# Cross-attention of 64 keys in parts of the matmul array: half-width scores, paired transposes, contexts in 64x64 quarters

## The chip, the cores and the metric

The kernel runs on one core of one Trainium2 chip. The metric is the device time in microseconds (us) of one execution. Engines are named as in the profile: PE is TensorE's matmul, PEld its weight load, DVE is VectorE, ACT is ScalarE, POOL is GpSimd, and SP is SyncE, which issues most DMAs.

## What is computed

The input x has 128 batches of 64 tokens with 128 features, and the context has the same shape. Each token of a batch attends to the context rows of its own batch, causally; then a mixture of experts follows (two of eight experts by a router, and one shared expert).

```
x = x + attention(layernorm(x), ctx, ctx)         # per batch: 64 queries, 64 keys, D = 128
    scores = q @ k.T * D ** -0.5;  masked above the diagonal;  softmax;  @ v
x = x + ffn(layernorm(x))
    logits = xt @ gate_w.T;  idx = top_k(logits + beta, 2);  weight = sigmoid(logits[idx])
    routed: sum over the two of weight * (silu(xt @ gate) * (xt @ up)) @ down
    shared: (silu(xt @ shared_gate) * (xt @ shared_up)) @ shared_down
```

## The kernel before

The 8192 tokens are worked in 16 groups of 512. A group is GT = 4 tiles of P = 128 tokens, so each tile holds two batches of T = 64. Each engine has its own program, a loop over iterations `it` in which it takes one step of several groups at once, and the engines meet only through semaphores. A semaphore `s_name` counts groups. In one iteration TensorE does, in this order (L1310 on): up matmul 0 of the shared expert of group it-4 (L1202), `attend(it-2)` (L1144), `transpose_xn2(it-3)` (L1154), gate matmul 0 (L1193), `transpose_probs(it-1)` (L1133), `route(it-3)` (L1163), `transpose_xn(it)` (L1113), the shared down projection of it-5 (L1214), up matmul 1 (L1202), `score(it)` (L1121, L1125), `ranks(it-3)` (L1174 to L1180) and gate matmul 1 (L1193).

Attention goes through these steps. `score` first puts a mask of 128x512 into PSUM bank A by a bf16 matmul with the identity, then adds four f32 matmuls of 128 tokens by 128 keys. Each tile of 128 tokens is so scored against both of its batches' keys, and the mask sets the other batch's half to -1e30. DVE takes the negative maximum of each row (L752), ACT the exponentials with their sums (L618). TensorE transposes the four 128x128 blocks of `probs` into bank C, ACT copies the 512 columns to `probs_T` (L626), and `attend` multiplies each by the 128 context rows of its tile into bank O. DVE's `residual` (L767) scales by the inverse sum and adds x. Router logits L and ranks R lie in bank O beside the contexts, at other times. `route` waits for the residual of the group that was attended in the same iteration (L1159), as it writes into bank O.

On DVE the residual stands behind `sum_up` and `shifts`, and ahead of the second layer norm's statistics. On ACT the exponentials stand behind the normalisation of a group two further back (L592).

SP loads a group's x, its context with features on the partitions (`c_T`, from a transposed copy in HBM) and its context rows (`c_sb`), three iterations ahead of use, in rings of 5 and 4 buffers (`load_x`, `load_c`); the contexts' buffers come free by `s_attended`. Then it stores a finished group. Routed tokens are scattered to lists by expert pair in HBM (GpSimd, L458). After the 16 groups a second stage gathers tiles of these lists and multiplies them with their experts (L1275, L1299).

A plain matmul of f32 is two instructions of each kind in the profile, so `score` has 8 besides the mask and `attend` 8. A transpose is one.

## Time and profile before

| | us |
|---|---|
| median of 3 runs | 423.53 (419.73 to 426.79) |
| the profiled execution, its own time | 422.82 |
| its span | 421.1 |
| PE busy, share of the span | 394.0, 94% |
| DVE busy | 300.8, 71% |
| ACT busy | 254.3, 60% |
| POOL busy | 267.0, 63% |

The page divides the span into 40 slices and gives each engine's busy share in tenths, and the clock that TensorE was granted, in tenths of 2.4 GHz. A timeline row merges instructions of one line; its first column is the start of the first and its second the time from there to the end of the last. As matmuls overlap, the distance from one row's start to the next row's start tells what an operation takes on the engine.

### The profile page before, as it was taken

To read this page: it belongs to the slowest core of one execution; us is meant where nothing else is said; L and a number is where in the kernel's file an instruction comes from. 1 tells how busy PE (TensorE), PEld (TensorE's weight loads), DVE (VectorE), ACT (ScalarE), POOL (GpSimd) and SP (SyncE) were. 2 spreads that over 40 slices of the span, in tenths; PEclk is the share of its full clock that TensorE was granted. 3 is DMA by queue.
4 is the path that set the end of the run, shared out by engine and by line. 5 is a ranking of instruction groups with operands and counts; after the bars stand their busy time and mean duration, and the time that the engine had idled before them with its cause. 6 is when DMAs were issued, how large, how long until landed. Compare 5 with 4: busy or idle time off the path is not lost.

```text
span 421.1 us, 10737 instructions
## 1 busy us (share of the span) xinstructions
PE 394.0 (94%) x3056; PEld 350.1 (83%) x3056; DVE 300.8 (71%) x1324; ACT 254.3 (60%) x554; POOL 267.0 (63%) x312
## 2 busy tenths in 40 slices
PE   7668999999999999989999999999999999999970
PEld 3556787778778887669999999989999999999970
DVE  3498799998999988776986666556667666666650
ACT  2568899999999994346566556553122565665520
POOL 7658788888888866617887888875200045555551
PEclk9699999999999999999999999999999999999995
DMA  8943344677444121244555666673332123432221
GB/s 241 342 126 102 102 126 127 214 239 229 126 131 156 59 60 58 73 116 98 92 82 81 91 82 91 90 111 55 50 78 55 35 26 47 53 39 26 22 25 12
DMA packets 61480, 41.76 MB, mean 99 GB/s; under 512 B 5688, under 2 KB 56384, under 8 KB 61424
## 3 DMA queue, kind: packets, MB, share of 16 engines
q1 hardware_dynamic: 49296, 30.69, 26.4%
q0 software_dynamic: 12128, 10.40, 17.4%
q8 instruction: 26, 0.43, 0.4%
q14 instruction: 30, 0.25, 0.2%
HBM read 24.17 MB, written 16.90 MB: 98 GB/s over the span
## 4 chain that ended last, share of the span: by engine, by line
PE 81%; POOL 4%; issue 4%; DVE 4%; DMA 3%; ACT 1%; SPq 1%; POOLq 0%; DVEq 0%; ACTq 0%
PE gu_pair L1275 30%; PE bank L1299 15%; PE bank L1202 7%; PE bank L1214 6%; PE bank L1193 6%; PE gu_pair L1144 3%; PE gu_pair L1125 3%; PE gu_pair L1163 3%; PE bank L1241 2%; PE gu_pair L1154 2%; DMA tile_in<-sorted_rows 1%; PE gu_pair L1113 1%; PE gu_pair L1133 1%; PE gu_pair L1180 1%; POOL rstd L417 1%
## 5 line engine op out<-in xcount | busy, mean ns | idle before, releaser
L509 POOL DMA_INDIRECT out<-t_out,tile_in x64 | 100.1, 1564 | 88.2 <-DVE t_out L1047 76.8
L1275 PE MATMUL gu_pair<-tile_T,W_slot 128*128 128x128 f32 x1024 | 124.8, 275 | 0.0
L1275 PEld LDWEIGHTS gu_pair<-tile_T,W_slot 128*128 128x128 f32 x1024 | 119.5, 192 | 0.1
L683 ACT ACTIVATE t_silu<-gu_pair 128x512 f32<-128x512 f32 (+1 forms) x78 | 46.4, 594 | 104.3 <-PE gu_pair L1275 96.2
L1007 DVE TENSOR_TENSOR t_hid<-t_silu,gu_pair 128x512 f32<-128x512 f32 (+1 forms) x78 | 53.0, 680 | 48.3 <-PE gu_pair L1275 47.9
L1299 PE MATMUL bank<-W_down,t_hid 128*128 (+1 forms) x620 | 82.7, 276 | 0.2 <-DVE t_hid L1007 0.2
L458 POOL DMA_INDIRECT sorted_rows<-rows,slot x64 | 63.6, 994 | 23.4 <-issue 16.8
L673 ACT ACTIVATE W_slot<-W 128x512 f32 x128 | 73.0, 621 | 6.1 <-issue 4.6
L1299 PEld LDWEIGHTS bank<-W_down,t_hid 128*128 128x128 f32 x620 | 75.4, 192 | 1.0 <-issue 0.8
L469 POOL DMA_INDIRECT left_in<-sorted_rows,left_index x27 | 26.5, 981 | 16.1 <-DVE left_index L926 8.2
L417 POOL TENSOR_TENSOR rstd<-var_eps,minus_half 128x4 f32<-128x4 f32 x32 | 33.0, 1032 | 5.7 <-DVE var_eps L738 5.3
L1202 PE MATMUL bank<-xn_T,shared_gu 128*128 128x512 f32 x64 | 33.2, 600 | 1.3 <-ACT silu_g L650 1.3
L592 ACT ACTIVATE rows<-x,shift,rstd 128x128 f32<-128x128 f32 x64 | 26.4, 483 | 13.0 <-DVE shift L744 13.0
L1193 PE MATMUL bank<-xn_T,shared_gu 128*128 128x512 f32 x64 | 33.2, 600 | 0.0
L1214 PE MATMUL bank<-shared_dn,hid 128*128 128x128 f32 x256 | 31.5, 276 | 0.9 <-DVE acc L845 0.9
L1214 PEld LDWEIGHTS bank<-shared_dn,hid 128*128 128x128 f32 x256 | 29.9, 192 | 1.5 <-issue 1.5
L1275 PE MATMUL gu_pair<-tile_T,W 128*128 128x128 f32 x216 | 26.4, 275 | 0.0
L424 POOL TENSOR_SCALAR xn<-x_sb,moments,rstd 128x128 f32<-128x128 f32 x32 | 25.2, 792 | 1.7
L618 ACT ACTIVATE probs<-gu_pair,neg_max 128x128 f32<-128x128 f32 x64 | 22.5, 364 | 4.9 <-DVE neg_max L752 4.8
L1275 PEld LDWEIGHTS gu_pair<-tile_T,W 128*128 128x128 f32 x216 | 25.2, 192 | 0.0
L767 DVE SCALAR_TENSOR_TENSOR x<-gu_pair,inv_sum,x_sb 128x128 f32<-128x128 f32 x64 | 18.0, 344 | 9.8 <-PE gu_pair L1144 9.8
L1241 PE MATMUL bank<-ident,tile_in 128*128 128x128 f32 x91 | 23.0, 276 | 1.7 <-DMA tile_in<-sorted_rows 1.7
(153 smaller groups left out, 637.0 us busy)
## 6 DMA issues: line engine op xcount, KB each, us to landing
tile_in<-sorted_rows SPq DMA_DIRECT2D x91, 66.5 KB, 2.0
x_sb<-x SPq DMA_DIRECT2D x16, 256.0 KB, 4.6
c_T<-ctx_cols SPq DMA_DIRECT2D x16, 256.0 KB, 2.9
c_sb<-ctx SPq DMA_DIRECT2D x16, 256.0 KB, 3.4
out<-acc SPq DMA_DIRECT2D x16, 256.0 KB, 3.4
sorted_rows<-padding SPq DMA_DIRECT2D x1, 2128.0 KB, 9.4
sorted_rows<-left_in SPq DMA_DIRECT2D x27, 66.5 KB, 2.1
sorted_rows<-rows,slot POOLq DMA_INDIRECT x64, 3.6
```

The lines of the kernel that those rows point to most:

```text
L417: e.tensor_tensor(rstd[:, n, g % 2], var_eps[:, n], minus_half[:], ALU.pow).then_inc(s_rstd[n], 1)
L458: e.indirect_dma_start(sorted_rows, bass.IndirectOffsetOnAxis(ap=slot[:, g % RR, i:i + 1], axis=0), rows[:, g % RR, i, :], None).then_inc( ...
L509: e.indirect_dma_start(out_flat, bass.IndirectOffsetOnAxis(ap=tile_in[:, tiles_of(i)[0] % NR, ID:ID + 1].bitcast(I32), axis=0), t_out[:, q ...
L673: r = e.activation(W_slot[:, q % TX, h], W[:, bass.ds(experts[q][h] * WN, WN)], ACT.Copy)
L683: e.activation(t_silu[:, 0:n * M], gate_up_pair[i % 2][0][:, 0:n * M], ACT.Silu).then_inc(s_t_silu, 1)
L1007: e.tensor_tensor(t_hid[:, i % 2, 0:n * M], t_silu[:, 0:n * M], gate_up_pair[i % 2][1][:, 0:n * M], ALU.mult).then_inc(s_t_hid, 1)
L1193: e.matmul((G0, G1)[m], shared_gu[:, 0, m * P:(m + 1) * P], xn2_T[:, g % RT], start=True, stop=True).then_inc(s_gate[m], 1)
L1202: e.matmul((U0, G0)[m], shared_gu[:, 1, m * P:(m + 1) * P], xn2_T[:, g % RT], start=True, stop=True).then_inc(s_up[m], 1)
L1214: r = e.matmul(Y[:, i * D:(i + 1) * D], hid[:, g % 2, m, i * P:(i + 1) * P], shared_dn[:, m], start=(m == 0), stop=(m == MC - 1), skip_gro ...
L1241: r = e.transpose(tile_pair[i % 2][:, h * P:(h + 1) * P], tile_in[:, n % NR, 0:D], ident[:])
L1275: r = e.matmul(bank[:, c:c + P], w, tile_T[:, i % TX, tile], start=True, stop=True, skip_group_check=True)
L1299: r = e.matmul(y, t_hid[:, i % 2, c:c + P], w, start=(m == 0), stop=(m == MC - 1), skip_group_check=True)
```

## The change

The code makes use of the batches of 64. Scores of a tile are computed for its own batch's 64 keys only: two matmuls per tile, of 64 tokens each, that write the lower and the upper 64 partitions of the same 64 columns, so that bank A holds 128x256 and the mask has 256 columns. ACT writes the exponentials so that tiles i and i+2 lie side by side in 128 columns, and one transpose turns both: two per group, into columns 0 to 255 of bank C, which ACT copies. A transposed block has the keys of tile n on partitions 0 to 63 and those of tile n+2 on 64 to 127. `attend` multiplies 64 keys by 64 tokens with 128 features, eight times: row half c of the array writes bank O (c = 0) or bank C (c = 1), and column half b the partitions of batch b. Context rows are loaded by two DMAs, each to 64 partitions. As bank C now holds contexts in the columns that the transposes write, `transpose_probs(g)` waits for the residual of group g-1.

```diff
-    ctx_rows = ctx_in.rearrange("b s d -> (b s) d").rearrange("(g t p) d -> g p t d", g=G, t=GT)
+    ctx_rows = ctx_in.rearrange("(g c m) k d -> g c k m d", g=G, c=2)
-        mask = sb("mask", [P, GT, P], BF16)
+        mask = sb("mask", [P, GT, T], BF16)
-        probs = sb("probs", [P, GT, P])
+        probs = sb("probs", [P, GT // 2, 2, T])
-        probs_T = sb("probs_T", [P, GT, P])
+        probs_T = sb("probs_T", [P, GT // 2, P])
-        L = O[:, 0:GT * E]
-        R = O[:, P:P + GT * Q]
+        scores = A[:, 0:GT * T]
+        attended = [half[:, c * 2 * D:(c + 1) * 2 * D] for c, half in enumerate((O, C))]
+        L = O[:, 2 * P:2 * P + GT * E]
+        R = O[:, 3 * P:3 * P + GT * Q]
...
-                e.dma_start(c_sb[:, g % RC], ctx_rows[g]).then_inc(s_c_in[g % RC], 16)
+                for c in range(2):
+                    e.dma_start(c_sb[c * T:(c + 1) * T, g % RC], ctx_rows[g, c]).then_inc(s_c_in[g % RC], 16)
...
-            e.affine_select(out=mask[:], in_=mask[:], compare_op=ALU.is_ge, fill=MASKED, base=0,
-                            pattern=[[0, GT], [-1, P]], channel_multiplier=1).then_inc(s_const, 1)
-            e.wait_ge(s_const, 7)
-            e.memset(mask[T:P, :, 0:T], MASKED).then_inc(s_const, 1)
+            e.affine_select(out=mask[0:T], in_=mask[0:T], compare_op=ALU.is_ge, fill=MASKED, base=0,
+                            pattern=[[0, GT], [-1, T]], channel_multiplier=1).then_inc(s_const, 1)
+            e.affine_select(out=mask[T:P], in_=mask[T:P], compare_op=ALU.is_ge, fill=MASKED, base=0,
+                            pattern=[[0, GT], [-1, T]], channel_multiplier=1).then_inc(s_const, 1)
...
-                    r = e.activation(probs[:, i], S[:, i], ACT.Exp, bias=neg_max[:, i:i + 1],
+                    r = e.activation(probs[:, i % 2, i // 2], S[:, i], ACT.Exp, bias=neg_max[:, i:i + 1],
...
-                r = e.activation(probs_T[:, :, :].rearrange("p t k -> p (t k)"), C, ACT.Copy)
+                r = e.activation(probs_T[:, :, :].rearrange("p n k -> p (n k)"), C[:, 0:GT * T], ACT.Copy)
...
-                    r = e.scalar_tensor_tensor(out=x2[:, g % RG, i], in0=O[:, i * D:(i + 1) * D],
+                    r = e.scalar_tensor_tensor(out=x2[:, g % RG, i], in0=attended[i // 2][:, i % 2 * D:(i % 2 + 1) * D],
...
-                e.matmul(A, ident_bf[:], mask[:, :, :].rearrange("p t k -> p (t k)"),
+                e.matmul(scores, ident_bf[:], mask[:, :, :].rearrange("p t k -> p (t k)"),
                          start=True, stop=False, skip_group_check=True)
                 for i in range(GT):
-                    s = slice(i * P, (i + 1) * P)
-                    r = e.matmul(A[:, s], xn_T[:, s], c_T[:, g % RC, s], start=False, stop=True, skip_group_check=True)
+                    for b in range(2):
+                        s = slice((2 * i + b) * T, (2 * i + b + 1) * T)
+                        r = e.matmul(scores[b * T:(b + 1) * T, i * T:(i + 1) * T], xn_T[:, s], c_T[:, g % RC, s],
+                                     start=False, stop=True, skip_group_check=True)
...
                 if g:
                     e.wait_ge(s_probs_T, g)
-                for i in range(GT):
-                    r = e.transpose(C[:, i * P:(i + 1) * P], probs[:, i], ident[:])
+                    e.wait_ge(s_x2, g)
+                for n in range(GT // 2):
+                    r = e.transpose(C[:, n * P:(n + 1) * P], probs[:, n].rearrange("p t k -> p (t k)"), ident[:])
...
-                e.wait_ge(s_c_in[g % RC], 16 * (g // RC + 1))
+                e.wait_ge(s_c_in[g % RC], 32 * (g // RC + 1))
...
-                for i in range(GT):
-                    r = e.matmul(O[:, i * D:(i + 1) * D], probs_T[:, i], c_sb[:, g % RC, i], start=True, stop=True)
+                for n in range(GT // 2):
+                    for b in range(2):
+                        for c in range(2):
+                            half = slice(c * T, (c + 1) * T)
+                            r = e.matmul(attended[c][b * T:(b + 1) * T, n * D:(n + 1) * D],
+                                         probs_T[half, n, b * T:(b + 1) * T], c_sb[half, g % RC, 2 * n + b],
+                                         start=True, stop=True, skip_group_check=True)
```

## Rows read from the trace of the kernel before

**Rows 1.** The page: busy time and share of each engine; the granted clock in slices.

```profile
PE 394.0 (94%) x3056; PEld 350.1 (83%) x3056; DVE 300.8 (71%) x1324; ACT 254.3 (60%) x554; POOL 267.0 (63%) x312
...
PEclk9699999999999999999999999999999999999995
```

**Rows 2.** Stretches: length, busy PE, PEld, DVE, ACT, POOL, clock, DMA share, GB/s.

```profile
0.00:52.10 52.10, 40.43 (x219) 29.18 (x220) 33.12 (x206) 31.96 (x89) 37.86 (x87) 0.90 0.60 185
...
52.10:150.60 98.50, 98.50 (x671) 77.57 (x670) 89.62 (x495) 91.33 (x221) 82.60 (x109) 1.00 0.50 152
...
185.20:421.10 235.90, 221.34 (x1957) 218.67 (x1955) 150.65 (x493) 113.89 (x206) 126.60 (x91) 0.98 0.42 62
```

**Rows 3.** Timeline of PE over one period; columns are start, us, engine, line.

```profile
71.55 0.38 PE L1121 MATMUL gu_pair<-mask,ident_bf 128*128 128x512 bf16 x1
71.76 1.05 PE L1125 MATMUL gu_pair<-c_T,xn_T 128*128 128x128 f32 x8
72.65 0.21 PE L1174 MATMUL gu_pair<-chosen,before_bf 128*128 128x112 bf16 x1
72.70 0.24 PE L1177 MATMUL gu_pair<-chosen,steps_bf 128*128 128x84 bf16 x3
72.80 0.45 PE L1180 MATMUL gu_pair<-list_next,last_row 128*128 128x112 f32 x2
...
74.82 1.05 PE L1144 MATMUL gu_pair<-c_sb,probs_T 128*128 128x128 f32 x8
75.71 0.60 PE L1154 MATMUL gu_pair<-ident,rows 128*128 128x128 f32 x4
76.15 1.02 PE L1193 MATMUL bank<-xn_T,shared_gu 128*128 128x512 f32 x2
77.01 0.60 PE L1133 MATMUL gu_pair<-ident,probs 128*128 128x128 f32 x4
77.44 0.96 PE L1163 MATMUL gu_pair<-router_T,xn_T 128*128 128x8 f32 x8
78.26 0.64 PE L1113 MATMUL gu_pair<-ident,xn 128*128 128x128 f32 x4
...
81.38 0.38 PE L1121 MATMUL gu_pair<-mask,ident_bf 128*128 128x512 bf16 x1
```

**Rows 4.** Timeline of the same period, ACT, DVE and PEld around the waits.

```profile
72.20 1.65 ACT L592 ACTIVATE rows<-x,shift,rstd 128x128 f32<-128x128 f32 x4 [0.67 <-DVE shift L744]
...
75.91 1.13 DVE L767 SCALAR_TENSOR_TENSOR x<-gu_pair,inv_sum,x_sb 128x128 f32<-128x128 f32 x4 [0.52 <-PE gu_pair L1144]
...
76.72 0.14 PEld L1133 LDWEIGHTS gu_pair<-ident,probs 128*128 128x128 f32 x1 [0.37 <-ACT probs L618]
```

**Rows 5.** Timelines elsewhere: 64 moving columns; half clock; an empty array.

```profile
180.92 0.78 PE L1226 MATMUL gu_pair<-ident,table 128*128 128x64 f32 x6
...
17.90 1.92 PE L1144 MATMUL gu_pair<-c_sb,probs_T 128*128 128x128 f32 x8
...
26.51 0.42 PEld L1154 LDWEIGHTS gu_pair<-ident,rows 128*128 128x128 f32 x4 [1.98 <-ACT rows L592]
26.52 0.66 PE L1154 MATMUL gu_pair<-ident,rows 128*128 128x128 f32 x4 [1.79 <-ACT rows L592]
```

**Rows 6.** Instructions of single lines: duration ns min/median/max, first and last start.

```profile
L626 ACT ACTIVATE probs_T<-gu_pair x10: 618/618/619, 61.0 to 149.7; 128x512 f32<-128x512 f32 x10
...
L654 ACT ACTIVATE tile_T<-bank x2: 277/277/277, 186.9 to 187.5; 128x128 f32<-128x128 f32 x2
...
L752 DVE TENSOR_REDUCE neg_max<-gu_pair x10: 672/675/690, 63.0 to 151.7; 128x4 f32<-128x512 f32 x10
...
L832 DVE TENSOR_REDUCE slot<-rank x16: 269/270/271, 33.3 to 176.1; 128x4 int32<-128x112 f32 x16
...
L310 SPq DMA_DIRECT2D c_sb<-ctx x16: 428/435/552, 1.8 to 125.5; - x16
...
DMA to landing us min/median/max: 3.2/3.4/5.0
```

More of the change, by code:

```diff
@@ L611, in exponentials @@
             def exponentials(g):
-                S = A.rearrange("p (t k) -> p t k", t=GT)
+                S = scores.rearrange("p (t k) -> p t k", t=GT)
                 e.wait_ge(s_row_max, g + 1)
@@ L747, in row_max @@
             def row_max(g):
-                S = A.rearrange("p (t k) -> p t k", t=GT)
+                S = scores.rearrange("p (t k) -> p t k", t=GT)
                 e.wait_ge(s_scores, g + 1)
```

## The prediction

> **What bounds the kernel now.** I read the page first. TensorE is busy for 94% of the span and its granted clock is full nearly everywhere [rows 1]. The table by stretches then separates three stages [rows 2]: a start of 52.1 us in which no engine is full, a steady part of 98.5 us in which TensorE is busy in every microsecond, and from 185.2 us on the expert tiles, which the change does not touch. The change can therefore act only in the first 185 us (between lie the last groups, with less and less attention). The steady part has ten equal periods: the mask matmul starts at 71.55 and again at 81.38 us, so one group of 512 tokens costs 9.83 us [rows 3]. The other engines are near their own limits in a period: DVE 8.96 us and ACT 9.13 us of 9.83 (tenths of the sums in [rows 2]). ACT loses 0.67 us more to a wait for DVE's shift, and DVE 0.52 us to a wait for the contexts [rows 4].
>
> The time of an operation on TensorE is the distance between starts, not its printed duration, since matmuls overlap. By [rows 3], scores take 72.65 - 71.76 = 0.89 us for 8 instructions (each f32 matmul is two), 0.111 us each; contexts 75.71 - 74.82 = 0.89 us; four transposes of probabilities 77.44 - 77.01 = 0.43 us; the mask 0.21 us. The same rows give a tail: eight context instructions last 1.05 us although the next group starts after 0.89, so a result is complete 0.16 us after the array is free for the next instruction.
>
> **What the change does to one period, term by term.**
> *Mask:* 256 columns instead of 512, half of 0.21: -0.105 us. *Transposes of the probabilities:* two instead of four, half of 0.43: -0.215 us. Both have one answer, as the instructions keep their form.
>
> *Scores:* 16 instructions with 64 stationary and 64 moving columns replace 8 with 128 and 128. Streaming is the same number of columns in all. The weight load decides: with only 8 moving columns, an f32 instruction of the router still costs (78.26 - 77.44) / 8 = 0.10 us [rows 3], and the six with 64 moving columns at 180.92 us fit within 0.78 us, their tail included, also 0.10 us each [rows 5]. So a full f32 weight load takes 0.10 us. By proportion, an estimate, one of 64 columns takes 0.05, and the scores take 16 x 0.05 = 0.80 us: -0.09. The ends: the fastest pairs of weight load and matmul in the trace are the three bf16 ones before L1180, (72.80 - 72.70) / 3 = 0.033 us each [rows 3], so 0.53 us and -0.36; if a load of 64 columns is not shorter, 16 x 0.10 = 1.60 us and +0.71. I take -0.09, the value between that the measured load time supports.
>
> *Contexts:* 16 instructions, each still with 128 moving columns, replace 8. Nothing in this trace works in a part of the array, so overlap is unknown. One after another they cost 16 x 0.111 = 1.78 us, +0.89. If all quarters overlapped, the dispatch bound above leaves 0.53 us, -0.36. I take a case between: the two instructions of one f32 matmul need the same quarter and cannot overlap each other, and instructions start in program order. Then the second half of a matmul can run only beside the first half of the next, and the eight matmuls take 8 x 0.111 + 0.111 = 1.00 us: +0.11. In other words, overlap of neighbours only pays back the doubled number of instructions.
>
> *Changes between the full array and its parts:* four in a period (into and out of scores, into and out of contexts). No row shows one. The lower bound is nothing; the upper is the tail of 0.16 us that must run out and a weight load of 0.10 that is no longer under it, 0.26 each. When the array is empty the first matmul starts 0.01 us after its weight load [rows 5], so nothing else has to be added. I take 0.13, the middle, for three of them, +0.39; the one after the contexts is discussed with the next term, since it hides the new wait. Ends 0 and +1.04.
>
> The Trainium skill's page "TensorEngine Tiling (Array Packing)", section Tiling Modes, speaks against the change here: changing the tiling mode drains TensorE. It gives no price, and no row of this trace shows one; with the rule taken as false this term would be zero and the sum 0.39 us lower.
>
> *The new wait:* probability transposes now write the columns of C that held the second half of the contexts, so they wait for the residual of the group before. Before, only the router behind them waited for it. DVE starts the residual at 75.91, as the contexts end, and takes 1.13 us, until 77.04 [rows 4]. TensorE has transposes (0.44) and a gate matmul (0.86) to do meanwhile, until 77.01 [rows 3]. The transposes of the probabilities thus start some 0.1 us after 77.04 instead of at 77.01 (a semaphore needs about 0.04 us, as from the contexts' end to the residual's start, and the weight load loses the lead that it had at 76.72 [rows 4]): +0.13 us, between 0.1 and 0.26. Behind it are queued the router, the next normalised x's transposes and the shared down projection; ACT is the one who waits for the last two groups' transposes. If leaving the quarters also costs a drain, the work between starts later and the wait is shorter by as much, so the fourth change is in this term.
>
> *Other engines:* ACT copies 512 columns in 0.618 us and 128 in 0.277 [rows 6], 0.89 ns a column. The copy of the probabilities loses 256 columns and the exponentials 4 x 64, together -0.45 us. DVE reduces 512 columns in 0.675 us and 112 in 0.270 [rows 6]: 256 columns fewer are -0.26 us. None of it is on the path while TensorE is full. It is what the others could follow with: DVE 9.83 - 0.52 - 0.26 = 9.05 us, ACT 9.13 - 0.45 = 8.68 us plus its wait. However fast the array gets, the period stays at about 9.05, a gain of at most 0.78.
>
> *Queues:* the context rows come in two DMAs of 64 partitions, one more issue of 0.435 us [rows 6] on SP per group, ahead of the x load and the store. Four buffers are in flight, SP idles for most of the period, and landing takes 3.4 us, so this costs nothing; without that cover it would be 0.435 a period. In the opening burst later loads move back by up to 5 x 0.435 us, of which I charge none to the end but keep 0 to +0.4 us. GpSimd builds a mask of half the size once, for nothing.
>
> **Sum.** -0.105 - 0.215 - 0.09 + 0.11 + 0.39 + 0.13 = +0.22 us a period. Scores and contexts lie on the full TensorE for some 12 groups (ten whole periods and a part on each side): +2.6 us. In the start, where a group's chain runs through DVE, ACT and TensorE in turn, up to 0.26 + 0.45 + 0.32 = 1.03 us a group comes off; much of that chain is GpSimd's, so I take half, for four groups: -2 us. In all +0.6 us on the profiled execution, whose own time is 422.8 us for a span of 421.1. The median of the three runs is 423.5, 0.7 above it; I forecast from the median: 424 us.
>
> **The rivals.**
> *The quarters do not overlap* (the change does not do what it says), on the slower side. Then contexts cost +0.89 instead of +0.11, the period +1.00, 12 groups +12 us. In the start the first contexts run at 1.2 GHz (eight instructions in 1.92 us instead of 1.05 [rows 5]), where the doubling costs more and eats the 2 us gained: about 436 us. It decides from the point where the sixteen context instructions take more than about 1.6 us together. For it: no row shows two matmuls streaming at once, and 0.111 us is what every 128-column f32 instruction costs here. Against it: the code gives each row half its own bank. If 64-column weight loads are not shorter either, another 0.8 x 12 = 10 us come on top: 446 us.
> *Everything overlaps* and changes between modes are nearly free. Per period -0.105 - 0.215 - 0.36 - 0.36 + 0.13 = -0.91 us; DVE ends it at -0.78, so 12 x 0.78 = 9.4 us, and with 2 to 3 us of the start: 412 us. For it: the separate banks and columns; against it: the pairs of instructions in one quarter, and sixteen f32 weight loads which alone come to 0.80 us if they run in turn.
> The Trainium skill's "TensorEngine Tiling (Array Packing)", section Overview, promises this one, up to 2x for each dimension of at most 64. The numbers of that page are none of this kernel's, and no row here shows the overlap.
> *The changes between modes cost their upper bound*, with overlap as in my forecast: four times 0.26, less what covers the wait: +0.52 on the sum, 12 x 0.52 = 6 us: 430 us.
>
> **How the numbers follow.** My forecast, partial overlap with moderate mode changes, 0.40: 424 us, its own range 418 to 429. No overlap 0.25 (436), with long weight loads also 0.05 (446). Full overlap 0.17 (412). Expensive changes 0.13 (430). A range from 412 to 438 leaves out nearly half of the fast case and all of the 446 and a part of the 436 case, about 2 in 10. Two per cent is 8.5 us, about what a measurement of this kernel tells from no change. Faster than 415: most of the full overlap and a little of the forecast's edge, 0.17. Slower than 432: no overlap and a fifth of the expensive changes, 0.31. The rest is 0.52.
>
> **What would show it.** In the period after: mask 0.11 us, two transposes 0.22; distance from first score to first rank matmul 0.8 us (0.53 full overlap, 1.6 long loads); distance from first context matmul to the transposes behind it about 1.1 us (0.5 to 0.6 full, 1.8 or more none). A gap of 0.1 to 0.3 us at each change of mode. The probability transposes released by DVE's residual, not by ACT's exponentials. A period between 9.9 and 10.2. The tile stage unchanged at 236 us. I am wrong if the array's parts behave outside these ends, or if the start moves by more than 3 us, through the clock's fall there.

## The result and the profile after

The changed kernel takes 417.24 us in the median of four runs (417.0 to 417.44), the kernel before 423.77 us in the median of four (419.73 to 426.79). The ratio is 0.989 with a 95% interval of 0.985 to 0.992. The kernel is about 1.1% faster: less than the two per cent that I had called a difference, but outside the interval of no change. I had forecast +0.6 us and it is -6.5. The profiled execution took 417.0 us, its span is 415.3. The size of the gain is less sure than its sign: the runs of the kernel before spread over 7 us and those of the changed one over 0.4, and when both were run again beside each other the medians were 420.94 and 417.37 us, 3.6 us apart.

The page of the changed kernel, the lines that answer to [rows 1]:

```profile
span 415.3 us, 11201 instructions
...
PE 389.3 (94%) x3279; PEld 330.5 (80%) x3280; DVE 297.4 (72%) x1324; ACT 247.5 (60%) x554; POOL 266.1 (64%) x312
...
PEclk9558999999999999999999999999999999999995
```

PE has 223 more matmul instructions and is busy 4.7 us less. The second to fourth slices of the granted clock stand at 5, 5 and 8, where [rows 1] have 6, 9 and 9.

The stretches of the changed kernel, which answer to [rows 2] (here cut at the masks just ahead of the first and the last scores of the steady part, and at the first matmul of the expert tiles):

```profile
0.00:51.04 51.04, 40.23 (x280) 24.98 (x281) 31.76 (x204) 29.93 (x89) 37.55 (x87) 0.77 0.65 189
...
51.04:146.51 95.47, 95.47 (x811) 64.34 (x810) 87.62 (x495) 86.92 (x220) 81.55 (x109) 1.00 0.53 157
...
183.27:415.30 232.03, 218.74 (x1949) 217.72 (x1949) 148.16 (x487) 112.35 (x202) 126.62 (x91) 0.98 0.42 62
```

The first scores of the steady part come 0.85 us earlier (52.10 before, 51.25 after), the last scores 3.9 us earlier (150.61 before, 146.71 after), the first matmul of the expert tiles 4.2 us earlier (187.45 and 183.27). From that matmul to the end it is 233.65 us before and 232.02 after. Nothing in that stage was changed, and in all the kernels profiled below it takes between 232.0 and 234.3 us. So 4.2 us of the 5.8 us between the spans are the change, 0.85 at the start and 3.05 in the steady part; the other 1.6 us lie within what this stage does by itself. These 4.2 us, and the 3.6 of the later runs, say better than the 6.5 what the change is worth.

TensorE over one period of the changed kernel, the timeline that answers to [rows 3]:

```profile
89.02 0.27 PE L1125 MATMUL gu_pair<-mask,ident_bf 128*128 128x256 bf16 x1
89.22 0.69 PE L1130 MATMUL gu_pair<-c_T,xn_T 128*64 128x64 f32 x16
89.84 0.22 PE L1186 MATMUL gu_pair<-chosen,before_bf 128*128 128x112 bf16 x1
...
91.16 1.02 PE L1214 MATMUL bank<-xn_T,shared_gu 128*128 128x512 f32 x2
92.11 0.67 PE L1154 MATMUL gu_pair<-c_sb,probs_T 64*64 64x128 f32 x16
92.71 0.66 PE L1166 MATMUL gu_pair<-ident,rows 128*128 128x128 f32 x4
93.20 1.02 PE L1205 MATMUL bank<-xn_T,shared_gu 128*128 128x512 f32 x2
94.12 0.41 PE L1140 MATMUL gu_pair<-ident,probs 128*128 128x128 f32 x2
94.47 1.06 PE L1175 MATMUL gu_pair<-router_T,xn_T 128*128 128x8 f32 x8
95.39 0.63 PE L1117 MATMUL gu_pair<-ident,xn 128*128 128x128 f32 x4
...
97.65 1.11 PE L1214 MATMUL bank<-xn_T,shared_gu 128*128 128x512 f32 x2
98.59 0.27 PE L1125 MATMUL gu_pair<-mask,ident_bf 128*128 128x256 bf16 x1
```

Read the distances between starts against those of [rows 3]. They add up to the two periods:

| from start to start, us | before | after | |
|---|---|---|---|
| mask to scores | 0.21 | 0.20 | half the columns, but a mode change is in it |
| scores to ranks | 0.89 | 0.62 | |
| ranks, gate, up, to contexts | 2.17 | 2.27 | 0.10 ahead of the quarters |
| contexts to transposes of normalised rows | 0.89 | 0.60 | |
| these transposes | 0.44 | 0.49 | 0.05 more behind the quarters |
| gate | 0.86 | 0.92 | the new wait |
| transposes of probabilities | 0.43 | 0.35 | 0.24 where nothing holds them; the rest is the wait for ACT's copy (L639) |
| router | 0.82 | 0.92 | its weight loads lost their lead in that wait |
| transposes of xn, down, up | 3.12 | 3.20 | waits for ACT |
| period | 9.83 | 9.57 | |

Over nine steady periods the mean falls from 9.848 to 9.541 us. Without what the waits for ACT cost in the last three lines a period would be 9.57 - 0.11 - 0.10 - 0.08 = 9.28 us. So TensorE's own work fell by 0.55 us, and only 0.31 arrived (0.26 between the two periods shown).

What took part of the rest back is in the rows of the other engines. The timeline of POOL in the changed kernel, over one period:

```profile
97.98 1.06 POOL L421 TENSOR_TENSOR rstd<-var_eps,minus_half 128x4 f32<-128x4 f32 x1
...
99.78 1.01 POOL L421 TENSOR_TENSOR rstd<-var_eps,minus_half 128x4 f32<-128x4 f32 x1
100.89 1.57 POOL L428 TENSOR_SCALAR xn<-x_sb,moments,rstd 128x128 f32<-128x128 f32 x2
102.64 1.10 POOL L462 DMA_INDIRECT sorted_rows<-rows,slot  x1 [0.18 <-issue]
...
106.58 0.96 POOL L462 DMA_INDIRECT sorted_rows<-rows,slot  x1 [0.30 <-issue]
107.56 1.06 POOL L421 TENSOR_TENSOR rstd<-var_eps,minus_half 128x4 f32<-128x4 f32 x1
```

From one power to the next it is 107.56 - 97.98 = 9.58 us, and the only gaps that the profile marks are those ahead of each indirect DMA (0.18 and three of 0.30), marked "issue": it waits for nobody. Its 266 us on the page and its 8.2 us busy in a period (a tenth of 81.55) look like slack, but the gaps of an issue cannot be filled. Before, the same list took 9.85 us, with 0.19 and 0.15 us of waits for ACT and DVE in it, 9.5 us of its own. GpSimd was nearly full already.

The ends of waits in the same period of the changed kernel (timelines of PEld, ACT and DVE), which answer to [rows 4]:

```profile
89.69 1.65 ACT L596 ACTIVATE rows<-x,shift,rstd 128x128 f32<-128x128 f32 x4 [0.82 <-DVE shift L748]
91.35 1.28 ACT L622 ACT_TABLE_LOAD   x1
...
95.20 1.28 ACT L653 ACT_TABLE_LOAD   x1
...
89.49 0.16 DVE L748 SCALAR_TENSOR_TENSOR shift<-moments,rstd 128x4 f32<-128x4 f32 x1 [0.20 <-POOL rstd L421]
...
92.84 1.13 DVE L771 SCALAR_TENSOR_TENSOR x<-gu_pair,inv_sum,x_sb 128x128 f32<-128x128 f32 x4 [0.16 <-PE gu_pair L1154]
...
94.09 0.20 PEld L1140 LDWEIGHTS gu_pair<-ident,probs 128*128 128x128 f32 x2 [0.69 <-ACT probs L622]
```

The chain runs: GpSimd's power, DVE's shift (L748), ACT's normalisation (L596), a load of ACT's function table, then the exponentials (L622), which end at 93.93. ACT now loses 0.82 us to the shift instead of 0.67; the rest of its period is work, and 2.56 us of that are the two table loads, one ahead of the exponentials and one ahead of the SiLU (L653). The kernel before has the same two, and no run took one away.

The new wait is for the residual, which ends at 93.97, 0.04 us after the exponentials. The last row names ACT, since the instruction that waits for the exponentials stands last, but in all ten steady periods it is the residual that ends last, by 0.02 to 0.28 us, and the transposes start 0.15 us behind its end (94.12 here), as they do wherever the residual is later by far (below). So DVE releases them; as it ends almost together with ACT, this costs TensorE only the 0.06 us of the gate's line.

How four quarters work shows in narrow windows of the changed kernel, contexts (L1154) alone; columns are the window, its length, busy PE and how many instructions touch the window, the same for PEld, clock, DMA share, GB/s:

```profile
92.10:92.15 0.05, 0.04 (x4) 0.04 (x4) 1.00 0.60 205
92.15:92.26 0.11, 0.11 (x4) 0.11 (x8) 1.00 0.90 312
92.26:92.37 0.11, 0.11 (x8) 0.11 (x8) 1.00 1.03 377
92.37:92.48 0.11, 0.11 (x12) 0.11 (x8) 1.00 0.49 169
```

Four matmuls begin in the first 0.05 us, 0.007 us apart, then none in the whole second window, then the next four: 16 instructions in four rounds, not in 16 steps of 0.111.

### The profile page after: what moved, and what is told of

It reads as the page before. It is cut to its first block, busy times and chain, and to the rows that moved or that the text cites. A ratio compares the mean times of both kernels' runs of the same rounds, so it can differ in the third digit from the quotient of the medians.

```text
span 415.3 us, 11201 instructions
## 1 busy us (share of the span) xinstructions
PE 389.3 (94%) x3279; PEld 330.5 (80%) x3280; DVE 297.4 (72%) x1324; ACT 247.5 (60%) x554; POOL 266.1 (64%) x312
## 4 chain that ended last, share of the span: by engine, by line
PE 52%; POOL 4%; issue 3%; DMA 3%; DVE 2%; SPq 0%; ACT 0%; POOLq 0%; DVEq 0%
PE gu_pair L1287 30%; PE bank L1311 15%; PE bank L1253 2%; POOL out L513 2%; PE bank L1226 2%; DMA tile_in<-sorted_rows 2%; PE bank L1214 1%; PE bank L1205 1%; DMA left_in<-sorted_rows,left_index 1%; POOL sorted_rows L462 1%; PE gu_pair L1175 1%; POOL left_in L473 1%; POOL rstd L421 0%; DVE acc L849 0%; DVE x L771 0%
## 5 line engine op out<-in xcount | busy, mean ns | idle before, releaser
L1214 PE MATMUL bank<-xn_T,shared_gu 128*128 128x512 f32 x64 | 34.2, 617 | 1.4 <-ACT silu_g L654 1.4
L596 ACT ACTIVATE rows<-x,shift,rstd 128x128 f32<-128x128 f32 x64 | 26.4, 483 | 14.3 <-DVE shift L748 14.3
L1205 PE MATMUL bank<-xn_T,shared_gu 128*128 128x512 f32 x64 | 33.6, 607 | 0.0
L1051 DVE SCALAR_TENSOR_TENSOR t_out<-bank,t_weight,t_part 128x128 f32<-128x128 f32 x64 | 22.5, 351 | 2.3
L962 DVE COPY tile_T<-bank 128x128 f32<-128x128 f32 (+1 forms) x76 | 23.2, 306 | 0.1
```

Source lines behind the costliest of these rows:

```text
L1205: e.matmul((G0, G1)[m], shared_gu[:, 0, m * P:(m + 1) * P], xn2_T[:, g % RT], start=True, stop=True).then_inc(s_gate[m], 1)
L1214: e.matmul((U0, G0)[m], shared_gu[:, 1, m * P:(m + 1) * P], xn2_T[:, g % RT], start=True, stop=True).then_inc(s_up[m], 1)
```

## The experiments

Ratios are against runs of the kernel before on the same chip, whose median was 420.9 to 423.3 us. "Period" is the mean over nine steady periods, 9.848 us before and 9.541 after.

| run | median, us | ratio to before, 95% | period, us |
|---|---|---|---|
| changed kernel, again | 417.37 | 0.988 (0.984 to 0.993) | 9.541 |
| contexts by quarter | 418.19 | 0.985 (0.979 to 0.991) | 9.536 |
| scores by half | 418.90 | 0.987 (0.981 to 0.993) | 9.604 |
| mask by halves | 417.29 | 0.983 (0.977 to 0.989) | 9.534 |
| before, scores in halves | 426.46 | 1.008 (1.004 to 1.011) | 10.069 |
| before, with the new wait | 424.91 | 1.007 (1.003 to 1.010) | 10.033 |
| one tile from GpSimd to ACT | 419.00 | 0.995 (0.992 to 0.997) | 9.626 |
| the same in the kernel before | 425.34 | 1.007 (1.004 to 1.011) | 10.006 |
| before, half of shared down | 419.81 | 0.997 (0.993 to 1.000) | 9.803 |
| the same with less ACT | 419.67 | 0.995 (0.991 to 0.999) | 9.711 |
| GpSimd lean | 415.93 | 0.987 (0.981 to 0.993) | 9.431 |
| one tile from GpSimd to DVE | 415.57 | 0.985 (0.980 to 0.990) | 9.486 |
| ACT's saving given back | 418.17 | 0.993 (0.990 to 0.996) | 9.566 |
| early shift | 421.69 | 1.000 (0.997 to 1.003) | 9.684 |
| early shift, tile to DVE | 420.93 | 0.997 (0.994 to 1.001) | 9.709 |
| these and early residual | 424.51 | 1.005 (1.002 to 1.007) | 10.051 |
| tile to DVE, early residual | 421.17 | 0.998 (0.996 to 1.001) | 9.950 |

### Do the quarters run at once, and in which order do they start?

In the changed kernel, all instructions of one quarter in a row:

```diff
-                for n in range(GT // 2):
+                for c in range(2):
                     for b in range(2):
-                        for c in range(2):
+                        for n in range(GT // 2):
```

> The changed kernel with the contexts' matmuls in another order: both of a quarter's matmuls (four instructions) one after another, then the next quarter. If each quarter has a queue of its own and dispatch goes on at 0.037 us, the last quarter gets its four instructions in the last 0.15 us and needs 0.44: the array is free some 0.2 to 0.3 us later, seen in front of the next transposes. If dispatch waits for the quarter to be free (the prediction's rule), four instructions take 0.44 us a quarter, and the contexts 1.4 to 1.8 us instead of 0.60. The period is GpSimd's 9.57 us in the first case, as TensorE has 0.4 us of slack.

Contexts to the next transposes: 0.62 us (0.60 in the changed kernel), and the period did not move. Neither expectation has it. The timeline and the narrow windows of this kernel:

```profile
73.08 0.69 PE L1154 MATMUL gu_pair<-c_sb,probs_T 64*64 64x128 f32 x16
73.70 0.66 PE L1166 MATMUL gu_pair<-ident,rows 128*128 128x128 f32 x4
```

```profile
73.07:73.13 0.06, 0.05 (x4) 0.05 (x4) 1.00 0.00 0
73.13:73.24 0.11, 0.11 (x4) 0.11 (x8) 1.00 0.00 0
```

Four matmuls begin within 0.05 us here too, though the program has the four instructions of one quarter ahead of those of the next. Four of one quarter would follow each other at 0.11; so these are of four quarters, and TensorE started three of them ahead of older instructions that waited for their own quarter. The Trainium skill's "TensorE: Matmul & The Clock Gate", section Part 3: Packing small matmuls, has matmuls start strictly in the order of the program; by that rule this order would cost about 1.4 us or more, as estimated before the run from 0.11 us a start, and the trace disagrees with it. The records name no quarter, so that the four are of four quarters is inferred from the rhythm: here their starts are 0.013 us apart, twice the 0.007 of the changed kernel, as twice as many instructions stand between one quarter's first and the next's.

The same for the scores, where halves share the moving side's rows:

```diff
-                for i in range(GT):
-                    for b in range(2):
+                for b in range(2):
+                    for i in range(GT):
```

> The changed kernel with the scores' matmuls ordered by column half: all four of the lower half (eight instructions), then all of the upper. Queues for each half: a half needs 8 x 0.053 = 0.43 us, the upper one starts at the eighth dispatch or so (0.3 us) and ends at 0.73 us, so the scores take 0.75 instead of 0.61 us. Dispatch that waits for the half: 0.86 us or more. If halves share the array without overlap, order makes no difference: 0.61.

Scores to ranks, timeline of this kernel:

```profile
71.48 0.97 PE L1130 MATMUL gu_pair<-c_T,xn_T 128*64 128x64 f32 x16
72.38 0.22 PE L1186 MATMUL gu_pair<-chosen,before_bf 128*128 128x112 bf16 x1
```

0.90 us instead of 0.62. The eight instructions of the lower half stand ahead of the upper's eight, and the first start of the upper half is 0.29 us after the first of the lower, when five of its eight have begun and three wait. In the order by quarter three of each quarter waited as well when the next quarter's first began, nine in all at the fourth, and only 0.02 us was lost. Both fit an array that takes instructions in order and lets three wait for each part of it; runs of four are then bridged whole, runs of eight are not. That is inferred from these two orders, and no length between was run. And the period grew by 0.06 only for 0.28 us more on TensorE. TensorE had slack; something else set the period.

### What does changing the mode cost?

The kernel before, its scores in column halves, with no column fewer:

```diff
-                    r = e.matmul(A[:, s], xn_T[:, s], c_T[:, g % RC, s], start=False, stop=True, ...)
+                    for b in range(2):
+                        h = slice(i * P + b * T, i * P + (b + 1) * T)
+                        r = e.matmul(A[b * T:(b + 1) * T, s], xn_T[:, h], c_T[:, g % RC, s], start=False, stop=True, ...)
```

> The kernel before with its 128x128 scores computed in column halves: 16 instructions of 64 stationary and 128 moving columns, keys, mask and all else unchanged. Column halves overlapping: the scores take 0.89 us as before plus what the two changes of mode cost; with 0.1 us each (as the gap behind the mask matmul grew in the changed kernel) the period is 9.9 to 10.05. With no overlap of column halves the scores take 1.78 us and the period is 10.7.

Timeline of this kernel around the scores:

```profile
74.70 1.02 PE L1205 MATMUL bank<-xn_T,shared_gu 128*128 128x512 f32 x2
75.87 1.09 PE L1127 MATMUL gu_pair<-c_T,xn_T 128*64 128x128 f32 x16
76.90 0.22 PE L1177 MATMUL gu_pair<-chosen,before_bf 128*128 128x112 bf16 x1
```

Sixteen instructions of 128 moving columns take 1.03 us where eight take 0.89, so the halves overlap almost wholly; one after another they would be 1.78. Up and mask ahead take 1.17 (1.07 before). The two differences make 0.24 us for going in and coming out, and the period grows by 0.22. In the kernel before, this comes through nearly in full (+0.76%).

In the changed kernel, the mask in column halves as well, so that it stands in the same mode as the scores:

```diff
-                e.matmul(scores, ident_bf[:], mask..., start=True, ...)
+                for b in range(2):
+                    e.matmul(scores[b * T:(b + 1) * T], ident_bf[:, b * T:(b + 1) * T], mask..., start=True, ...)
```

> The changed kernel with the mask put in by two matmuls in the same column halves as the scores, so that the change of mode lies ahead of the mask and not between mask and scores. If the 0.21 us from the mask's start to the scores' start is 0.107 of streaming and 0.10 of mode change, the mask now takes 0.11 to 0.15 us and the matmul ahead of it 0.10 longer. If the mask matmul of 256 columns simply takes 0.21, two of them take as long or longer. The time is GpSimd's either way: 417 us.

Mask to scores falls from 0.20 to 0.13 and the scores to 0.56, but the up matmul ahead takes 1.04 instead of 0.94: the 0.10 us of the entry has only moved. The period is 9.534.

### What does the new wait cost?

The kernel before with nothing but the wait:

```diff
                 if g:
                     e.wait_ge(s_probs_T, g)
+                    e.wait_ge(s_x2, g)
```

> The kernel before with only the new wait added: the transposes of the probabilities wait for the residual of the group before. The prediction's term: +0.13 us a period (9.96), +1.5 us in all. Rival: the wait costs nothing, since the residual ends as the gate matmul ends; period 9.83 to 9.86.

Timeline of this kernel:

```profile
74.99 1.02 PE L1194 MATMUL bank<-xn_T,shared_gu 128*128 128x512 f32 x2
76.03 0.63 PE L1134 MATMUL gu_pair<-ident,probs 128*128 128x128 f32 x4
76.49 0.96 PE L1164 MATMUL gu_pair<-router_T,xn_T 128*128 128x8 f32 x8
```

The gate takes 1.04 us instead of 0.86 and the transposes 0.46; the period grows by 0.19, within my bounds of 0.1 to 0.26 and 0.06 above the value taken. The transposes start 0.15 us after the residual's end (75.88) here too, and the exponentials end 0.6 us before it. In the changed kernel DVE's residual begins 0.36 us sooner after the first context matmul, where DVE waits for it (1.09 us before, 0.73 after), and the wait is nearly covered. Taking the wait itself away was not tried: the transposes would overwrite contexts in bank C that DVE is still reading, and no other bank is free.

### Which engine holds the period at 9.55?

*ACT's part.* Half of GpSimd's share of the first normalisation goes to ACT, in the changed kernel and in the one before:

```diff
-                for i in range(GT // 2):            # GpSimd, normalise_x
+                for i in range(1):
-                for i in range(GT // 2, GT):        # ACT
+                for i in range(1, GT):
```

> The changed kernel with GpSimd normalising one tile of x instead of two; ACT takes three instead of two (about 0.39 us more for ACT, 0.79 us less for GpSimd in a period). Theory G, GpSimd is what now bounds a period at 9.57 us: the period falls to TensorE's own sum, 9.2 to 9.3 us, the time by 3 to 5 us against the changed kernel, to 412 to 414 us. Rival L, the chain from DVE's shift through ACT's exponentials to TensorE's transposes bounds it: ACT's longer work makes the period 9.6 to 9.8 us and the time stays at 417 or rises to 419.

> The same shift of one tile from GpSimd to ACT in the kernel before, where TensorE is full. Theory G: the period stays 9.83 us, and only the start may gain 1 to 2 us. Rival L: ACT's 0.39 us more brings it to 9.5 us plus its wait, so the period becomes 9.9 to 10.1 us and the time 1 to 3 us longer.

It made both slower, the periods by 0.09 and 0.16 us. In the changed kernel GpSimd now stands still, and ACT's chain is the later one; its timeline of POOL:

```profile
90.11 0.21 POOL L442 TENSOR_SCALAR sigmoid<-tanh_l 128x32 f32<-128x32 f32 x1 [0.87 <-ACT tanh_l L645]
```

That an engine is freed does not show that it did not bind when the edit loads the next one. The pair only says that ACT's chain lies within about 0.3 us of the period in both kernels.

*Is TensorE the only limit before?* The kernel before without half of the shared down projection (one of its two halves of the hidden features is left out):

```diff
-                    for m in range(MC):
+                    for m in range(1):
```

> The kernel before with half of the shared down projection left out (8 of its 16 matmul instructions, 0.89 us of TensorE in a period), and nothing else touched. TensorE's own sum is then 8.94 us. Theory G: the period stops at GpSimd's 9.57 us, so of 0.89 us only 0.26 are gained. The floor that the prediction took from DVE would let it fall to 9.31 us. With no other bound it would be 8.94.

Down falls from 1.78 us to 0.89, and the period by 0.04, in turn 9.57 and 10.05. Its timeline at the end of the down projection:

```profile
78.37 1.06 PE L1214 MATMUL bank<-shared_dn,hid 128*128 128x128 f32 x8
79.80 1.12 PE L1202 MATMUL bank<-xn_T,shared_gu 128*128 128x512 f32 x2 [0.37 <-ACT silu_g L650]
```

The up matmul behind it writes a bank that ACT frees only by its SiLU; in the neighbouring period it waited 0.71 us. Time taken from TensorE there is put back by ACT at once. The gain of the change is on the other side of that point, where the contexts release DVE's residual: from the first contexts to the residual it is 1.09 us before and 0.73 after. The shorter scores do not bring DVE's maxima forward in the same way: from the first scores to the maxima it is 1.11 us at 71.76 before and 1.21 at 89.22 after. That the place decides is argued from these rows; no run takes the same time off at both places.

With the same lean down projection, ACT also gets less to do (exponentials of every second key after the first group, and half of the copy to `probs_T`; both leave part of the attention out):

```diff
-                    r = e.activation(probs[:, i], S[:, i], ACT.Exp, ...)
+                    k = 1 if g == 0 else 2
+                    r = e.activation(probs[:, i, 0:P:k], S[:, i, 0:P:k], ACT.Exp, ...)
...
-                r = e.activation(probs_T[:, :, :]..., C, ACT.Copy)
+                k = GT if g == 0 else GT // 2
+                r = e.activation(probs_T[:, 0:k]..., C[:, 0:k * P], ACT.Copy)
```

> The kernel before with half of the shared down projection left out, as in the earlier run, and now ACT's columns cut as the change cuts them: exponentials of every second key and a copy of half of the transposed probabilities (the rest left out after the first group). The period of the earlier run was 9.80 us on average, alternating between 9.57 and 10.05, with TensorE waiting for ACT's silu. If ACT was the cause, the period is now GpSimd's 9.57 us throughout. If not, it stays at 9.80.

9.711 against 9.803: some 0.09 us for about 0.45 us of ACT. The period again alternates, 9.58 and 9.8 to 9.97. With less on TensorE and on ACT together, every second period comes to GpSimd's 9.58 and none lower.

*Was it ACT's saving that made the change pay?* The changed kernel, ACT copying 256 and 128 columns more per group, into a buffer that nobody reads:

```diff
+                e.activation(again[:, 0:2]..., C[:, 0:GT * T], ACT.Copy)
+                e.activation(again[:, 2], C[:, 0:P], ACT.Copy)
```

> The changed kernel with two extra copies on ACT (256 and 128 columns of PSUM, 0.46 us a period), about what the change took off ACT. If the saving on ACT was needed for the gain, since the chain through ACT stood at 9.8 us before, the period goes back to 9.7 to 9.8 us although TensorE's and GpSimd's work is unchanged. If ACT has nothing to do with it, it stays at 9.58.

The period is 9.566 (+0.025). The gain of the steady part does not depend on ACT's shorter exponentials and copies; that rival is out there. The whole kernel is 0.8 us slower than the changed one on the same chip (418.17 and 417.37), of which 0.25 is the ten periods.

*GpSimd.* The changed kernel without GpSimd's normalisation of tile 1 after the first group (that tile keeps stale values):

```diff
-                for i in range(GT // 2):
+                for i in range(GT // 2 if g == 0 else 1):
```

> The changed kernel in which GpSimd normalises one tile of x instead of two after the first group (the second tile's values stay those of the first group: left out, not moved), so GpSimd's period is 0.79 us shorter and no other engine has more to do. If GpSimd bounds the changed kernel at 9.58 us, the period falls until the next bound, TensorE's own sum of 9.2 or the ACT chain at some 9.25: 9.2 to 9.35 us, the time to 413 to 415. If not GpSimd but the chain through ACT bounds it, the period stays at 9.5 to 9.6.

The period falls to 9.431, alternating between 9.27 and 9.6. So GpSimd did hold the changed kernel, but by 0.11 us only: every second period reaches the 9.28 that TensorE's own work takes, and the others stay where they were. And the same work given to DVE, which seems to have some room; the changed kernel's waits over ten periods (total, times, longest):

```profile
DVE x L771 <- PE gu_pair L1154: 1.6, 7, 0.4
...
DVE shift L748 <- POOL rstd L421: 1.3, 5, 0.3
```

```diff
-                for i in range(GT // 2):            # GpSimd, normalise_x
+                for i in range(1):
...
+            def normalise_one(g):                   # DVE, right after shifts(it, 0)
+                if g:
+                    e.wait_ge(s_xn_transposed, g)
+                e.tensor_scalar(xn[:, 1], x_sb[:, g % RX, 1], moments[:, 0, 1, 0:1], rstd[:, 0, g % 2, 1:2],
+                                ALU.subtract, ALU.mult).then_inc(s_normal[3], 1)
```

> The changed kernel with DVE normalising the second tile of x in place of GpSimd, behind its shift: GpSimd 0.79 us less, DVE 0.2 to 0.3 us more. With GpSimd as the bound and DVE's chain at about 9.05 us: period 9.3 to 9.4, time 414 to 416. If DVE's longer chain decides: 9.6 or more and no gain.

415.57 us (414.89 to 417.19), the fastest kernel here, ratio 0.985; its interval overlaps that of the changed kernel, so the further 1 to 2 us are likely and not shown. Its timelines of PE and POOL:

```profile
78.95 0.27 PE L1135 MATMUL gu_pair<-mask,ident_bf 128*128 128x256 bf16 x1
...
88.22 0.27 PE L1135 MATMUL gu_pair<-mask,ident_bf 128*128 128x256 bf16 x1
```

```profile
78.88 0.35 POOL L443 TENSOR_SCALAR sigmoid<-tanh_l 128x32 f32<-128x32 f32 x1 [0.55 <-ACT tanh_l L646]
...
88.13 0.21 POOL L443 TENSOR_SCALAR sigmoid<-tanh_l 128x32 f32<-128x32 f32 x1 [0.28 <-ACT tanh_l L646]
```

88.22 - 78.95 = 9.27, while GpSimd now waits for ACT. The next period is 9.55, others like it up to 9.78. DVE's room is gone: over the same ten periods its waits sum to 0.7 us instead of 2.9.

### What holds every second period?

The last kernel's two kinds of period differ on TensorE in three places, each of them at or behind a wait for ACT: 0.33 instead of 0.24 us for the transposes of the probabilities, 0.91 instead of 0.82 for the router, 0.95 instead of 0.86 for the up matmul. ACT in turn waits 0.82 us for DVE's shift in the long one and 0.49 in the short one, and DVE waits for nobody. In all these kernels ACT loses 0.5 to 1.0 us to that shift. In the changed kernel, GpSimd's second power goes between the scatters and DVE's shift ahead of the router's steps:

```diff
                 for i in range(GT):                 # GpSimd, scatter(g)
+                    if i == 2 and 3 <= g + 5 < G + 3:
+                        powers(g + 2, 1)
                     e.indirect_dma_start(
...
+                if 3 <= it < G + 3:                 # DVE, ahead of bias_logits and choose
+                    shifts(it - 3, 1)
```

> The changed kernel with the same work in another order: GpSimd computes the second norm's power between the second and third scatter instead of after the fourth, and DVE makes the shift ahead of the choice of experts instead of behind it, so ACT no longer waits 0.8 us for it. If GpSimd's own 9.58 us of work is the only bound, the period stays at 9.54 to 9.58. If the chain over two periods is the bound, it falls to 9.2 to 9.4.

And with the tile given to DVE as well:

```diff
+            normalise_one(it)    # as above, DVE; and powers and shifts moved as in the diff before
```

> The same order together with DVE normalising one tile of x in place of GpSimd, so that both suspects are relieved. If they are all that stands above TensorE's own sum, the period falls to 9.2 to 9.25 us and the stage ends 3 us earlier than in the changed kernel; time 412 to 414. If TensorE still waits for another chain: 9.4 to 9.5 and 415 to 416.

ACT's wait for the shift is gone, and the kernel is slower than the changed one all the same (9.684; 421.69 us); none of the expectations has that. The timeline of PE in the first of them shows what is late now:

```profile
93.88 1.02 PE L1207 MATMUL bank<-xn_T,shared_gu 128*128 128x512 f32 x2
95.22 0.41 PE L1142 MATMUL gu_pair<-ident,probs 128*128 128x128 f32 x2 [0.31 <-DVE x L773]
```

1.34 us from gate to transposes instead of 0.92, released by DVE's residual: this is the new wait, and here it binds. ACT's exponentials are done at 93.29 us, but DVE begins the residual at 93.94 and ends at 95.07. With the tile on DVE the same gap is 1.35.

> The changed kernel itself, for comparison on this chip: a period of 9.54 us, 417 to 418 us, a ratio of 0.985 to 0.992 to the kernel before.

The changed kernel run again is as it was: 417.37 us, period 9.541, tile stage 232.2 us. Its two medians differ by 0.13 us.

If the late residual is the trouble, it could go ahead of `sum_up` in DVE's order (with one more buffer for x2, and the weights behind the maxima):

```diff
-        RX, RC, RR, RG, RT = 5, 4, 7, 4, 4
+        RX, RC, RR, RG, RT = 5, 4, 7, 5, 4
...
+                if 2 <= it < G + 2:                 # now ahead of sum_up(it - 6)
+                    residual(it - 2)
```

> The kernel with the early shift and DVE's tile of x, and on DVE the residual now ahead of the sum of the shared output (with a fifth buffer for x2), the routing weights' sum behind the row maximum. If the new wait for the residual was what held the period at 9.71 us because DVE came to it late, TensorE's gate matmul before the transposes falls from 1.35 to 0.9 to 1.0 us and the period to 9.3 to 9.4; time 413 to 415. If DVE is simply full, the period stays at 9.6 to 9.7.

> The changed kernel with DVE's tile of x and the early residual, but the shift where it was. The chain over two periods from the residual through the second norm to ACT's exponentials gets shorter by up to 0.3 us, 0.15 a period: 9.3 to 9.45 us against 9.49, time 413 to 415.5. If the residual only waits for TensorE there, nothing changes: 9.49.

10.051 and 9.950 us, longer than in the kernel before; neither expectation has it. In the first the gate is back to 0.92, but from the router to the transposes of the next x it is now 1.28 us: these wait for ACT's half of that x, and ACT waits 0.68 us for the shift of the first norm, which now stands behind the residual. In the second ACT waits 0.97 us for the other shift. Each of the four orders moved the last wait to another pair of engines and found nothing below 9.54. What sets the longer of the alternating periods stays open: the rows show a ring through DVE's shift, ACT's normalisation, table load and exponentials, TensorE's transposes and back, over two periods, but no experiment opened it. The table loads, 2.56 us of ACT's period, are the longest link that no run touched.

## Why the prediction was wrong

*The step that failed is the contexts.* I took 1.00 us on two assumptions, that the two instructions of one f32 matmul cannot overlap and that instructions start in the order of the program, so that only neighbours overlap. The first may be true of a pair, but there are four quarters, and four pairs run side by side: 0.60 us, -0.29 instead of +0.11. The second is false where quarters differ (contexts by quarter, 0.62). My lower bound of 0.53 was close.

*Scores:* 0.62 instead of 0.80, for the same reason: I had priced 16 weight loads in turn, and those of two halves overlap. -0.27 instead of -0.09.

*Changes of mode:* there are drains, as I took against a sum without them, but they are smaller. Going in costs 0.10 us twice, coming out 0.05 behind the contexts, and coming out of the scores is in their 0.62, as is the slower first round of the quarters in the contexts' 0.60; together 0.25 instead of 0.39, and 0.24 for one pair alone in the kernel before. The rule of the Trainium skill's "TensorEngine Tiling (Array Packing)", section Tiling Modes, holds, with this price.

*Mask and transposes:* nearly as forecast. The mask's 0.20 us less the entry of 0.10 leave 0.10, and two transposes take 0.24 instead of 0.43 where nothing holds them (I had 0.215).

*The new wait:* +0.19 alone in the kernel before (0.13 forecast), +0.06 in the changed one, since faster contexts bring the residual forward. Its releaser is DVE's residual, as I had named, by some hundredths of a us ahead of ACT's exponentials.

*The sum:* of my +0.22 a period, contexts and scores are 0.58 too dear, the mode changes 0.14, the wait 0.07. Corrected: +0.22 - 0.58 - 0.14 - 0.07 = -0.57 us, the 0.55 of the profile.

*The floor under it:* I had DVE's 9.05 us as the next limit and left GpSimd out, as its 82.60 us busy in [rows 2] looked like the least. Back to back it needs 9.58 us. This was a second error, and it worked against the first: of the 0.55 us only 0.31 arrived. Of the other 0.24 GpSimd holds 0.11 (GpSimd lean); the rest is the chain through DVE's shift and ACT, which stays open. DVE's own floor was too low too: in the period shown it is 9.54 less its waits of 0.20 and 0.16 us, 9.2. The rival "everything overlaps" was the right mechanism; its 412 us were too low by this floor, 10 x (0.78 - 0.31) = 4.7 us, and by the start.

*The start:* -0.85 us instead of -2. The two kernels' windows there, before first and after second:

```profile
20.00:30.00 10.00, 6.14 (x45) 4.95 (x45) 9.23 (x60) 6.54 (x23) 5.60 (x15) 1.00 0.52 140
```

```profile
20.00:30.00 10.00, 7.89 (x57) 5.38 (x55) 8.71 (x67) 6.00 (x20) 6.05 (x16) 0.50 0.83 242
```

In these ten microseconds TensorE had its full clock before and 1.2 GHz after, and the mean granted clock of the start is 0.77 instead of 0.90. That the start's gain was eaten there is what the rows suggest, and no run isolates it. Other traces bear it out: among the kernels built from the one before, the first scores of the steady part come at 50.54 us where the mean clock of the first 50 us is 0.93 (the new wait alone), at 52.10 and 51.74 where it is 0.90 (before; half of shared down), and at 54.05 to 55.74 where it is 0.83. All traces of changed kernels have 0.76. A difference of 0.85 us in the start is thus no measure of the change.

*The tile stage* is unchanged within its own spread, as forecast. *The queues* cost nothing visible: the split loads of context rows land as before, and no wait for them shows in the steady part.

## What to carry to other kernels

Matmuls in quarters of the array run at once even in f32, and with up to four instructions of one quarter in a row. For 64x64 work expect the time of a quarter of the instructions plus about 0.3 us: here four rounds of 0.11 us became 0.60, and 0.10 and 0.05 stand on the two sides. When the bounding engine gets cheaper, list for every other engine the time from one iteration's first instruction to the next's, less its waits on others: gaps that belong to its own instructions (an issue of an indirect DMA) count as work, however idle the page shows it. Relieving the fullest of them gives little when the next are as close as here (0.11 us for 0.79 us of GpSimd's work). And where the time is taken off can decide what arrives: 0.89 us of TensorE ahead of a bank that ACT frees gave 0.04, 0.55 us elsewhere in the period gave 0.31. When a wait names several semaphores, compare the ends of all that it waits for, and not only the name in the row.

## What the runs showed of the hardware

- Four 64x64 quarters run f32 matmuls at once (changed kernel): starts 0.007 us apart, rounds of four every 0.11 us, the first 0.16, 16 instructions in 0.60 us where eight of the full array take 0.89. Two column halves do the same, in rounds of 0.058 us for 64 moving columns.
- TensorE starts matmuls of other parts of the array ahead of older ones that wait for theirs, over runs of four (0.62 us instead of 0.60); over runs of eight it does so only when three are left waiting (0.90 instead of 0.62).
- Entering a part mode costs 0.10 us and leaving it 0.05 or a little more, 0.24 for a pair in a kernel bound by TensorE; doing a neighbour in the same mode moves the entry and does not remove it.
- GpSimd's indirect DMA costs its engine 0.96 us and a gap of 0.30 each, 1.26 us per issue, and its power of 128x4 values 1.03 us; four issues and two powers are 7 of the 9.58 us.
- ACT loads a function table for 1.28 us ahead of the exponentials and again ahead of the SiLU, in every period.
